# Experts' rows kept whole in DRAM at their slots, loaded as plain tiles, and gate sums from heads and x1: one change to a three-part decoder layer on one core

## The reference, cut

```python
x = _layernorm(x + attn_ref(x, ...))           # Mamba-like mixer, chunked scan: x1
x = _layernorm(x + xattn_ref(x, ctx, ctx, ...)) # 16 heads of 8, softmax over 256 keys: x2
x = _layernorm(x + ffn_ref(x, gate, w0, w1, wo)) # 8 experts, the best 2 of each token
# inside ffn_ref
gate_logits = inputs @ gate_kernel                      # [B, S, 8]
weights, selected = top_k(gate_logits, 2); weights = softmax(weights)
hidden_e = silu(rows_of_e @ w0[e]) * (rows_of_e @ w1[e])   # rows sorted by expert
out[token] = sum over its 2 experts of weight * (hidden_e @ wo[e])
```

## Time and profile before

| | |
|---|---|
| median of 3 runs | 476.38 us (475.7 to 478.96) |
| the profiled execution | 477.21 us, span 475.9 us, mean granted clock 0.750 |
| busy: PE, DVE, ACT, POOL | 77%, 65%, 49%, 51% of the span |
| DMA moved | 41.47 MB, HBM written 13.71 MB |

### The profile page before, as it was taken

How to read it: one execution, slowest core, us unless ns; L and a number is a source line. 1 busy time by engine, 2 the same in 40 slices (tenths; PEclk the granted TensorE clock), 3 DMA queues, 4 the chain that set the end, 5 groups by cost and what they waited for, 6 DMA issues and landing times.

```text
span 475.9 us, 7878 instructions
## 1 busy us (share of the span) xinstructions
PE 367.5 (77%) x2489; PEld 253.7 (53%) x2489; DVE 311.5 (65%) x794; ACT 232.3 (49%) x455; POOL 241.0 (51%) x305
## 2 busy tenths in 40 slices
PE   2997777797889778888756696945699999999900
PEld 1675555564435445444322333434489999999800
DVE  3647344777677888889898837346276666666635
ACT  2775544332555655454727364400266665666504
POOL 3730677633334442513565748270746667674416
PEclk9998557555565979697859555555599999999965
DMA  8832315424504040407223322001111111121052
GB/s 287 316 107 68 102 35 165 145 77 98 138 32 138 6 133 4 134 8 220 60 68 106 86 93 79 12 3 55 44 35 52 45 48 48 49 48 35 29 187 88
DMA packets 40183, 41.47 MB, mean 87 GB/s; under 512 B 4912, under 2 KB 33904, under 8 KB 40144
## 3 DMA queue, kind: packets, MB, share of 16 engines
q1 hardware_dynamic: 35888, 34.13, 23.6%
q0 software_dynamic: 3392, 5.23, 4.1%
q10 hardware_dynamic: 864, 1.61, 0.9%
HBM read 26.98 MB, written 13.71 MB: 86 GB/s over the span
## 4 chain that ended last, share of the span: by engine, by line
PE 60%; DVE 24%; POOL 5%; issue 5%; ACT 3%; DMA 2%; DVEq 0%; POOLq 0%; ACTq 0%
PE banks L897 12%; DVE nm L1091 7%; PE banks L801 6%; PE banks L921 5%; PE banks L753 4%; PE banks L909 4%; DVE topf L1153 4%; PE banks L701 3%; PE banks L624 3%; PE banks L721 3%; PE banks L922 2%; PE banks L812 2%; PE banks L844 2%; PE banks L744 2%; PE banks L711 2%
## 5 line engine op out<-in xcount | busy, mean ns | idle before, releaser
L1421 ACT ACTIVATE probs_all<-banks 128x1024 f32<-128x1024 f32 x64 | 65.4, 1022 | 66.5 <-PE banks L753 65.7
L1091 DVE TENSOR_REDUCE nm<-banks 128x4 f32<-128x1024 f32 x64 | 78.0, 1218 | 14.2 <-PE banks L744 13.4
L897 PE MATMUL banks<-w_split,scores_in 128*128 x234 | 65.3, 416 | 0.7 <-DVE scores_in L1264 0.7
L801 PE MATMUL banks<-probs_all,vals 128*9 128x256 f32 x512 | 53.9, 503 | 2.8 <-DVE avT L1107 2.1
L1620 POOL DMA_INDIRECT y_dram<-avT,scatter_u x39 | 38.3, 983 | 32.4 <-DVE avT L1270 32.1
L753 PE MATMUL banks<-scores_in 32*128 32x256 f32 x256 | 41.6, 410 | 16.7 <-DVE nm L1091 14.5
L1613 POOL DMA_INDIRECT scores_in<-x_dram,gather_i x39 | 37.7, 968 | 25.3 <-DVE scatter_u L1238 13.7
L897 PEld LDWEIGHTS banks<-w_split,scores_in 128*128 128x128 f32 x234 | 42.6, 196 | 8.2 <-issue 1.2
L1252 DVE TENSOR_TENSOR ctx_in<-ctx_in,banks 128x512 f32<-128x512 f32 x39 | 26.8, 688 | 30.1 <-ACT ctx_in L1466 30.1
L744 PE MATMUL banks<-scores_in 32*128 32x256 f32 x256 | 41.3, 408 | 6.2 <-DVE nm L1091 6.1
L753 PEld LDWEIGHTS banks<-scores_in 32*128 32x128 f32 x256 | 25.9, 246 | 35.4 <-DVE nm L1091 25.5
(11 more groups left out here) (224 smaller groups left out, 795.6 us busy)
## 6 DMA issues: line engine op xcount, KB each, us to landing
scores_in<-k_dram SPq DMA_DIRECT2D x32, 128.0 KB, 2.8
scores_in<-q_dram SPq DMA_DIRECT2D x32, 128.0 KB, 3.0
ctx_in<-in_L_ffn_w SPq DMA_DIRECT2D x16, 256.0 KB, 2.7
cs_wide<-cs_dram SPq DMA_DIRECT2D x14, 256.0 KB, 3.5
k_dram<-split_qk SPq DMA_DIRECT2D x8, 256.0 KB, 2.5
q_dram<-split_qk SPq DMA_DIRECT2D x8, 256.0 KB, 2.2
ctx_in<-in_L_ffn_wo SPq DMA_DIRECT2D x8, 256.0 KB, 2.7
x_in<-in_x SPq DMA_DIRECT2D x4, 256.0 KB, 5.2
```

The costliest lines, as they stand in the source:

```text
L801: m = TE.matmul(AV[32 * j:32 * j + HD + 1, r % 2 * S:(r % 2 + 1) * S], vals[:, TPS * b + k, GR * j + r, :], probs(2 * quad + j // 2)[:, j ...
L897: m = TE.matmul(bank(2 * slot + j), xT[:, i % XT, xh, :], all_weights[:, c + j * FF:][:, bass.ds(expert_at[i], FF)], start=n == 0, stop=n ...
L1091: V.tensor_reduce(most, maxima_of(n).rearrange("p (j k q) -> p j k q", j=2, k=TPS), AX_X, ALU.max, negate=True).then_inc(s["nmax"], 1)
L1421: C.activation(probs(n).rearrange("p j k q -> p (j k q)"), EXPS, ACT.Exp, scale=SCALE).then_inc(s["probs"], 1)
```

## The change

The slot table goes. `x2_dram` now has one row of 130 floats (x2, the result's place, the weight) for each slot of each expert, 16,384 rows and 128 spare ones. In detail:

- ACT clears these rows by 17 DMAs in steps -40 to 8 (`clear_rows`), 16 of 1024 rows each.
- SP copies x2 of a batch twice into `x2_rows` in SBUF (the last batch by ACT), POOL adds code and weight (`weights`), and after `rank_chosen` POOL scatters the four tiles (`scatter_rows`), in all eight batches.
- `place_last`, its products, the table's read and the gather indices go. `expert_order` has no gathers: SP reads the tile's first row into a register and issues a plain load of 128 rows into `xg`, a ring of 6 that is free when `y_add` of tile i-6 has come, since code and weight are read from it in `down`.
- In `down` DVE makes the tile's scatter rows itself, by two small instructions ahead of its add.
- The gate's sums no longer wait for x2: with the weights centred over D, sums of x1 (turned in `turn_gated`) and of oT are added in PSUM, and the gap is multiplied by rs2 later (`scale_gaps`). That is four products a batch in place of two. `turn_gate` and `gate_heads` make the centred weights once.
- Lags are changed in the mixer and behind the attention; `LEADS_IN` is 34, so there is one step more.

```diff
-XG, AHEAD = 8, 6
+XG = 6
-LEADS_IN = 33
+LEADS_IN = 34
-LAGS = (('load_queries', 12), ('query', 11), ('turn_x1', 10), ('mix_norm', 9), ('mix_residual', 7), ('mix_project', 7), ('turn_mixed', 6))
+LAGS = (('load_queries', 14), ('query', 13), ('turn_x1', 12), ('mix_norm', 11), ('mix_residual', 9), ('mix_project', 9), ('turn_mixed', 8))
...
-    (lambda b: (("rank_chosen", b), ("place_chosen", b)), 15),
+    (lambda b: (("rank_chosen", b), ("place_chosen", b)), 12),
+    (whole("x2_norm"), 7),
     (lambda b: (("gate_top", b), ("choose", b)), 9),
-    (whole("split_x2"), 8),
-    (whole("x2_norm"), 7),
+    (whole("scale_gaps"), 11),
+    (whole("weights"), 12),
+    (whole("scatter_rows"), 13),
     (whole("out_project"), 6),
     (whole("turn_heads"), 5),
+    (whole("turn_gated"), 0),
...
-SOONER = (10, 9, 7, 6, 5, 4, 3, 2, 0)
+SOONER = (7, 9, 5, 8, 8, 8, 5, 4, -2, 3, 2, 0)
+CLEAR_AT = range(-40, -40 + 3 * (CLEARS + 1), 3)
...
+            for i in range(SLOT_TILES):
+                tile_at = SY.value_load(tiles_at[0:1, i:i + 1], min_val=0, max_val=NE * T)
+                q.wait_ge(s["y_add"], i - XG + 1)
+                SY.dma_start(xg[:, i % XG, :], x2_dram[bass.ds(tile_at, P), :]).then_inc(a[f"g{i % XG}"], 16)
...
+            def gate_top(b):
+                q.wait_ge(s["xgT"], b + 1)
+                q.wait_ge(s["steps_v"], GATE_SET)
+                freed(b).wait()
+                for k in range(TPS):
+                    sums = follow_up(b)[:, S + k * NE:S + (k + 1) * NE]
+                    TE.matmul(sums, x1_gT[:, b % 2, k * P:(k + 1) * P], gate_c[:, :], start=True, stop=False)
+                    q.wait_ge(s["oT"], b + 1)
+                    m = TE.matmul(sums, oT[:, k * P:(k + 1) * P], gate_o[:, :], start=False, stop=True)
...
             def down(i):
+                code = xg[:, i % XG, CODE_AT:CODE_AT + 1]
+                q.wait_ge(s["down_mm"], i + 1)
+                own.step(V.scalar_tensor_tensor(slots[:, i:i + 1], code, 0.0, spare_rows[:, i:i + 1], ALU.is_equal, ALU.mult))
+                own.settle()
+                own.step(V.scalar_tensor_tensor(scatter_u[:, i:i + 1], code, -1.0, slots[:, i:i + 1], ALU.add, ALU.add))
+                own.settle()
                 q.wait_ge(s["y_half"], i + 1)
...
+            def scatter_rows(b):
                 q.wait_ge(s["placed"], b + 1)
+                q.wait_ge(s["weight"], b + 1)
+                if b < B - 1:
+                    q.wait_ge(a["rows_in"], 16 * TOPK * (b + 1))
+                else:
+                    q.wait_ge(s["steps_a"], LAST_X2)
+                q.wait_ge(a["x2_out"], 16 * TOPK * TPS * b)
+                q.wait_ge(a["rows_clear"], ROWS_ALL)
                 for i in range(TOPK * TPS):
+                    G.indirect_dma_start(x2_dram[:, :], bass.IndirectOffsetOnAxis(ap=place_u[:, b % 2, i:i + 1], axis=0),
+                                         x2_rows[:, b % 2, i // TPS, i % TPS, :], None).then_inc(a["x2_out"], 16)
```

More of the change, by code:

```diff
@@ L228, in expert_order @@
 def expert_order():
-    for i in range(AHEAD):
-        yield "gather", i
     for i in range(TURNED_AHEAD):
@@ L234, in expert_order @@
     for i in range(SLOT_TILES + DOWN_LAG):
-        if i + AHEAD < SLOT_TILES:
-            yield "gather", i + AHEAD
         if i < SLOT_TILES:
@@ L260 @@
     "q_mm max_mm nmax nm_split nm_t nm_out exp_mm probs av_mm av_lo av_hi x1b heads_t o_norm o_t oT wo_mm "
-    "r2 ln2_var ln2_in ln2 x2 x2_t x2T gate_mm logit gap chosen rank_mm counted placed w_hi w_lo "
+    "r2 ln2_var ln2_in ln2 x2 xg_mm xgT gate_mm logit gap gap_exp weight_in weight chosen rank_mm counted placed w_hi w_lo "
     "xg_t xT_hi xT_lo up_mm sil hid turn_mm hsT_hi hsT_lo down_mm y_half y_add "
@@ L292, in build @@
         wq, wo, bo, d_skip, rms_w, gate = (rest[:, c] for c in (W_Q, W_O, B_O, D_SKIP, RMS_W, GATE))
-        of_expert, limit, spare_rows, iota, column = (rest[:, c] for c in (MASK, LIMIT, SPARE, IOTA, COLUMN))
+        of_expert, limit, spare_rows, iota, tile_rows = (rest[:, c] for c in (MASK, LIMIT, SPARE, IOTA, TILE_ROWS))
         x_in = sb("x_in", [P, NT, D])
@@ L316, in build @@
         mv2 = sb("mv2", [P, TPS, 2])
-        rs2 = sb("rs2", [P, TPS])
+        rs2 = sb("rs2", [P, 2, TPS])
+        gate_c = sb("gate_c", [P, NE])
+        gate_o = sb("gate_o", [P, NE])
+        gate_b = sb("gate_b", [P, NE])
+        x1_gT = sb("x1_gT", [P, 2, S])
         logit = sb("logit", [P, TPS, NE])
@@ L402, in build @@
         yT = w_in[:, 0:TPS * 2 * P].rearrange("p (k c l) -> p k c l", k=TPS, c=2)
-        x2T = cT[:, 1, :]
+        woT, boT = (cT[:, 1, i * P:(i + 1) * P] for i in range(2))
         x2 = x_in
@@ L450, in build @@
         W_FIRST, W_KV, W_REST_N = 16, 16, 16 * 2
-        INIT = 16 * 3
+        INIT = 16 * 2
+        ROWS_ALL = 16 * (CLEARS + 1)
         MAX_ROWS = 16
@@ L1149, in gate_top, with scale_gaps @@
                 own.settle()
-                q.wait_ge(s["consts_g"], ROWS_SET)
-                V.tensor_tensor(row_src[:, b, :, :, 1], top[:, :, 1].unsqueeze(1).to_broadcast([P, TOPK, TPS]),
-                                top[:, :, 0].unsqueeze(1).to_broadcast([P, TOPK, TPS]), ALU.subtract).then_inc(s["gap"], 1)
+                own.step(V.tensor_tensor(gap_d[:, b % 2, :], top[:, :, 1], top[:, :, 0], ALU.subtract))
                 own.step(V.tensor_copy(topf[:, :, :], topi[:, :, :]))
                 own.settle()
+            def scale_gaps(b):
+                q.wait_ge(s["ln2"], b + 1)
+                q.wait_ge(s["gap_exp"], b - 1)
+                V.tensor_tensor(gap[:, b % 2, :], gap_d[:, b % 2, :], rs2[:, b % 2, :], ALU.mult).then_inc(s["gap"], 1)
             def choose(b):
@@ L1416, in maxima_out, with clear_rows, x2_norm, scale_gaps @@
                 C.activation(nm_rows[:, :], MISC[0:2 * AH, 0:S], ACT.Identity).then_inc(s["nm_out"], 1)
+            def clear_rows(n):
+                q.wait_ge(s["consts_g"], ZEROS_SET)
+                rows = NE * T // CLEARS if n < CLEARS else P
+                part = x2_dram[n * NE * T // CLEARS:][0:rows].rearrange("(p n) c -> p n c", p=P)
+                C.dma_start(part, zeros[:, :].unsqueeze(1).to_broadcast([P, rows // P, ROW])).then_inc(a["rows_clear"], 16)
+            def x2_norm(b):
+                if b < B - 1:
+                    return
+                q.wait_ge(s["x2"], TPS * (b + 1))
+                q.wait_ge(a["x2_out"], 16 * TOPK * TPS * (b - 1))
+                C.activation(x2_rows[:, b % 2, :, :, 0:D], x2[:, TPS * b:TPS * b + TPS, :].unsqueeze(1).to_broadcast([P, TOPK, TPS, D]),
+                             ACT.Identity).then_inc(s["steps_a"], 1)
+            def scale_gaps(b):
+                q.wait_ge(s["gap"], b + 1)
+                q.wait_ge(s["weight"], b - 1)
+                C.activation(parts[:, b % 2, :], gap[:, b % 2, :], ACT.Exp).then_inc(s["gap_exp"], 1)
             def exps(n):
@@ L1452, in slots_of_experts @@
             def slots_of_experts():
-                q.wait_ge(s["steps_pe"], GAPS_MM)
-                C.activation(slot_w[:, 0, :], bank(4)[:, 0:SLOT_TILES], ACT.Exp).then_inc(s["steps_a"], 1)
                 C.preload_act_table_set("silu_and_others")
@@ L1646, in pool_program @@
                     middle[stage](*at)
-            experts = dict(gather=gather, down=down)
+            experts = dict(down=down)
             for stage, *at in expert_order():
```

259 lines of the change are left out of this document (115 added, 144 removed).

## The result

The changed kernel takes 493.94 us (median of four runs, 491.59 to 497.13), the kernel before 476.04 beside it: a ratio of 1.037 with a 95% interval of 1.030 to 1.045. It is slower, by about 18 us. The profiled execution took 494.24 us, its span 492.6.

A forecast was written before the change was run, and what follows sets the result against it. No engine was taken to bound the whole: PE in the expert tiles, PE and DVE alternately before, then one long chain. 14.6 - 13.5 + 2.5 + 0.1 + 3 - 4.5 = +2.2 gave 479 us, range 463 to 493.

The forecast's parts named there:

- Experts' loads: Expert tiles: loads waiting for y_add of six tiles ago stall PE 0.86 us, 17 times; +14.6 us (7.8 to 23.1).
- estimate of 2.15 us: Experts' slot loads: landing time for 66,560 bytes by the Trainium skill page, giving a 0.81 us stall and a 13.8 term.
- A cast ... ends when four weight pieces ... are done: Middle: three DVE casts held by rows of POOL weight pieces get their time back; -13.5 us (-15 to -5).
- In its place the root rs2 of the next batch stands behind the scatters: Middle, POOL: DVE's x2_norm waits up to 1.5 us for rs2 in two or three batches; +2.5 us (0 to 10).
- nearly gone: Middle, POOL: the pile of pieces behind the scatters nearly vanishes, with four steps, some 10 us, between scatters and cast.
- the middle: Between first and last exponent: forecast of -13.5 for casts, +2.5 for the rs2 wait and +0.1 for the gate.
- POOL becomes the queue: Rival, middle: POOL fills, its pile reaches x2_norm and cast, most of the 13.5 returns as rs2 waits; about 491, chance 0.27.
- The rival with the experts at half clock: Rival, experts' stage: PE's idles drop its clock and passes double at most, up to +90 us; chance 0.04.
- Gate: Middle, PE: no more waits for x2 (-5.2 us) against two more products a batch (5.3 us); together +0.1.
- Clears and the mixer's order: Mixer's stage: clears through ACT's queue, mostly hidden, and DMA traffic delaying keys, queries and maxima rows; +3 us (-3 to +9).
- Last batch: Routing of the last batch: first expert turn at about 331.9 us instead of 336.43; -4.5 us (-8 to 0).

The follow-up runs named there:

- experiment 1: Changed kernel with ten places in the experts' ring instead of six; 480.39 us, ratio 1.011 to the kernel before the change.
- Experiment 11: Changed kernel with wide clears, scatter_rows at lag 17 instead of 13 and seven ring places instead of six; 468.22 us, ratio 0.985.
- after: The changed kernel itself as traced, with no further edit; 493.94 us, ratio 1.037 to the kernel before the change.
- 10: Kernel before the change with ranks and places at lag 12 instead of 15, so scatters precede the next batch's rs2; 473.68 us, ratio 0.996.
- 3: Changed kernel with scatter_rows at lag 15 instead of 13, behind rs2 of the next batch; 488.51 us, ratio 1.027.
- Experiment 9: Kernel before the change with the cast of the indices written as a reduction over one element; 476.88 us, ratio 1.002.
- 7: Changed kernel with scatter_rows at lag 17 instead of 13, behind the next batch's choice; 486.13 us, ratio 1.020.
- 2: Changed kernel with a wider zero tile, so clears move pieces of 4160 bytes instead of 520; 489.52 us, ratio 1.034.
- 4: Changed kernel with LEADS_IN, LAGS and TILE_LAGS (the mixer's order) of the kernel before the change; 495.95 us, ratio 1.042.
- 12: Changed kernel with wide clears and the mixer's order of the kernel before the change; 491.08 us, ratio 1.027.

## Why the prediction was wrong

It said 479 where 493.94 was measured, 0.9 us above its range. By its own steps:

**Experts' loads, +14.6: right in cause and nearly in size, in part by luck.** 13.0 measured, and experiment 1 gives back 12.1 of it. 17 turns behind the first two wait for their load, as many as forecast. But the median landing is 1.8 us, not 2.2; with 1.8 and 0.1 the same sum gives 0.46 us a stall and 7.8 in all, the lower bound. The idle recorded at those turns is 0.16 to 1.18 us, 7.0 in all, while two passes take mostly 6.1 to 6.6 us as forecast; some loads landed later (up to 3.1 us), and the runs don't say where the rest of the growth comes from. The prediction's estimate of 2.15 us by the Trainium skill ("DMA: Bandwidth & Descriptors", Anatomy of one DMA) stands on figures that the page gives for a transfer issued by GpSimd; this one is issued by SP, and landed in 1.8. Experiment 11 confirms the margin: a place more adds a pass, 2.8 us, and no stall is left.

**"A cast ... ends when four weight pieces ... are done", -13.5: right in its mechanism.** The casts of the indices fell to 0.27 us and less (after, 10), and came back when the pile was put ahead of them (3). Experiment 9 shows which operations are held.

**"In its place the root rs2 of the next batch stands behind the scatters": named, and mis-sized. This is the step that failed.** I priced it at DVE's wait alone, up to 1.5 us in two or three batches, +2.5 with bounds of 0 to 10. The trace shows waits of up to 4.12, 10.9 in all in four. The size of one comes out of the prediction's own terms. POOL was to need 5.0 + 1.3 + 1.0 = 7.3 us from the places to rs2; it needed 8.86 (256.76 to 265.62), because one piece more stood ahead of the scatters. DVE was to be there after three steps of 1.9 to 2.7 us; it was there after 4.8 (at 261.54), with exponents 1.7 us apart and a granted clock of 1.00 from 255 to 263 us. 8.9 - 4.8 is the 4.1 that was measured.

Behind that wait the term had the maxima, but not the copy of avT, for which PE waits (12.3 us in four times; 5.7 in 7). The pile that I called "nearly gone" meets `x2_norm` itself, two scalings that POOL's pieces hold as they held the cast (2.51 us for 0.60), but 7 has the same hold and a short middle. So the middle gave 2.0 us and not 10.9, and with the scatters behind the next batch's choice it gives 11.8 (7), near what was forecast for it.

It was the rival "POOL becomes the queue", at 491 and 0.27, that came: "the pile reaches x2_norm", though not the cast, and "most of the 13.5 comes back as waits for rs2". Its condition was worked out for POOL filled at 2.25 us a step or less; POOL is busy 51.91 of 83 us, so it needed no full POOL, only the wrong order on it. The rival with the experts at half clock did not come, their stage ran at 0.97.

**Gate, +0.1: not separated.** Waits of PE for x2 are gone, and PE is busy 7.4 us more from 226 to 309 us, but these windows do not hold the same steps; no run takes the gate's products alone.

**Clears and the mixer's order, +3: right part, too small.** 7.4, inside the bounds of the term. I named the DMA share and priced ACT's issues; the cost is in the landing of others' transfers, 7.0 us instead of 3.5 for the sums, and 5.4 us of the path came from the size of the pieces (2). No cost of the new order shows in front: 1.5 us between 4 and after, 0.1 between 12 and 2, both within what near kernels differ by.

**Last batch, -4.5: right in direction**, -2.2 in the table.

Measured against the forecast of each term, the middle missed by 8.9 us, the front by 4.4 and the last batch by 2.3, all upward; the experts' stage came out 1.6 below. Each of these lies inside the bounds of its term, and the range was narrower than those bounds together.
